# A fused attention and expert layer on one core: transposed projections, 512-column fp32 score matmuls and once-transposed tokens

## What is computed

```python
x = L0_attn_x                       # (8, 1024, 128)
xn = _layernorm(x, axis=-1)
x = x + _L0_attn_ref(xn, ...) + _L0_ffn_ref(xn, ...)
```

```python
q, k, v = (qkv[:, :, 0], qkv[:, :, 1], qkv[:, :, 2])
k = _layernorm_noaffine(k)          # over the 8 features of each head
inter = jnp.einsum('bhde,bthe->bthd', S, q_c)
scores = jnp.einsum('bthd,bshd->bhts', q_c, k_c)
scores = jnp.where(causal, scores, 0.0)
intra = jnp.einsum('bhts,bshd->bthd', scores, v_c)
S = S + jnp.einsum('bthd,bthe->bhde', v_c, k_c)
```

```python
xn = xhat[None, :, :] * ln_g[:, None, :] + ln_b[:, None, :]
h = jax.nn.relu(jnp.einsum('etd,efd->etf', xn, w1) + b1[:, None, :])
y = x[None, :, :] + jnp.einsum('etf,edf->etd', h, w2) + b2[:, None, :]
```

## Time and profile before

| | |
|---|---|
| median of 3 runs | 646.09 us (638.41 to 648.07) |
| profiled execution, its own time | 645.7 us |
| its span | 644.1 us |
| PE, PEld busy | 549.8 us (85%), 434.6 us (67%) |
| DVE, ACT, POOL busy | 396.2, 274.7, 334.3 us |
| mean granted TensorE clock | 0.919 |

### The profile page before, as it was taken

The page is one execution under the profiler, slowest core; times in us unless marked ns, Lnnn a source line. Parts: engine busy times, 40 slices in busy tenths (PEclk is TensorE's granted clock), DMA queues, the critical chain, the costliest instruction groups (busy, mean ns, idle before and its releaser), DMA issues.

```text
span 644.1 us, 18105 instructions
## 1 busy us (share of the span) xinstructions
PE 549.8 (85%) x5829; PEld 434.6 (67%) x5830; DVE 396.2 (62%) x1080; ACT 274.7 (43%) x586; POOL 334.3 (52%) x361
## 2 busy tenths in 40 slices
PE   0798588888888889889889888888979999999993
PEld 0454366666666667667767666666659899998993
DVE  5887845655556556556556456566446677777773
ACT  1688334444444443443443444444433444434341
POOL 3555135554553554544543554555105777777775
PEclk9999857997999898898897898897579999999998
DMA  9695000100100000000000000010203444444440
GB/s 231 188 292 165 0 18 19 31 26 14 31 26 13 29 29 8 29 29 8 29 29 8 29 29 8 29 31 9 52 17 51 63 59 62 56 63 60 59 58 4
DMA packets 49807, 32.08 MB, mean 50 GB/s; under 512 B 8296, under 2 KB 46440, under 8 KB 49776
## 3 DMA queue, kind: packets, MB, share of 16 engines
q0 software_dynamic: 13840, 13.93, 12.7%
q1 hardware_dynamic: 32816, 17.73, 10.5%
q10 hardware_dynamic: 3120, 0.01, 0.3%
HBM read 14.07 MB, written 18.10 MB: 50 GB/s over the span
## 4 chain that ended last, share of the span: by engine, by line
PE 76%; ACT 9%; issue 5%; DVE 3%; DMA 3%; SPq 2%; ACTq 1%; POOL 0%; POOLq 0%; DVEq 0%
PE bank L1127 13%; PE bank L1108 10%; PE bank L1246 10%; PE bank L1065 10%; PE bank L1238 5%; ACT pr L538 4%; PE bank L1096 4%; PE bank L1230 3%; PE bank L1118 3%; PE bank L1232 3%; PE bank L1231 3%; DMA resid<-in_L_attn_x_dram 3%; PE bank L1098 3%; PE bank L1141 3%; ACT q L507 2%
## 5 line engine op out<-in xcount | busy, mean ns | idle before, releaser
L343 POOL TENSOR_SCALAR_AFFINE_SELECT pr<-pr 128x512 f32<-128x512 f32 x128 | 86.4, 682 | 151.5 <-ACT pr L538 150.8
L767 DVE TENSOR_TENSOR pr<-bank,causal 128x512 f32<-128x512 f32 x128 | 87.9, 687 | 121.8 <-PE bank L1108 121.4
L410 POOL DMA_INDIRECT out_dram<-qs,idxe x72 | 112.3, 1559 | 55.5 <-DVE qs L955 29.5
L1108 PE MATMUL bank<-qqt,kkt 32*128 32x128 f16 x1024 | 91.9, 228 | 29.9 <-ACT pr L538 28.2
L543 ACT ACTIVATE y<-bank 128x128 f32<-128x128 f32 x64 | 17.7, 277 | 196.9 <-PE bank L1127 196.9
L1108 PEld LDWEIGHTS bank<-qqt,kkt 32*128 32x128 f16 x1024 | 52.4, 97 | 67.9 <-issue 28.8
L538 ACT ACTIVATE pr<-bank 128x512 f32<-128x512 f32 x128 | 77.5, 606 | 22.3 <-PE bank L1108 22.1
L1127 PE MATMUL bank<-pr,vz 128*32 128x128 f32 x2048 | 79.9, 304 | 0.4 <-POOL pr L343 0.4
L354 POOL DMA_INDIRECT slots_d<-xq,idxq x64 | 64.7, 1010 | 22.5 <-POOL idxq L349 13.0
L1246 PE MATMUL bank<-w2t,pr 128*128 x576 | 76.0, 275 | 0.0
L1065 PE MATMUL bank<-wqkv,xt 128*128 128x128 f32 x384 | 67.1, 329 | 9.8 <-ACT xt L501 9.8
(11 more groups left out here) (170 smaller groups left out, 942.1 us busy)
## 6 DMA issues: line engine op xcount, KB each, us to landing
slots_d<-zrow POOLq DMA_DIRECT2D x8, 594.0 KB, 6.4
xs<-slots_d SPq DMA_DIRECT2D x72, 66.0 KB
resid<-in_L_attn_x_dram SPq DMA_DIRECT2D x8, 512.0 KB, 6.5
out_dram<-res SPq DMA_DIRECT2D x16, 256.0 KB
state<-in_L_ffn_w_dram SPq DMA_DIRECT2D x8, 256.0 KB
res<-in_L_ffn_w_dram SPq DMA_DIRECT2D x8, 256.0 KB
out_dram<-qs,idxe POOLq DMA_INDIRECT x72
slots_d<-xq,idxq POOLq DMA_INDIRECT x64, 2.3
```

The costliest lines, as they stand in the source:

```text
L343: pool.affine_select(out=pr_v[:, i % 2, g, :, :], in_=pr_v[:, i % 2, g, :, :], compare_op=ALU.is_ge, fill=0.0, base=0, pattern=[[0, J], [1 ...
L410: pool.indirect_dma_start(out_rows, bass.IndirectOffsetOnAxis(ap=idxe[:, a:a + 1].bitcast(U32), axis=0), ye[:, a, :], None, bounds_check=N ...
L767: nc.vector.tensor_tensor(pr_v[:, a, g, :, :], SC[1][:, :].rearrange("p (j t) -> p j t", j=J), bcast(causal[:, :], 1, J), ALU.mult)\
L1108: last = mm(SC[g % 2][:, j * P:(j + 1) * P], kkt[32 * g:32 * (g + 1), i % 2, j, :], qqt[32 * g:32 * (g + 1), i % 2, j, :], start=True, sto ...
```

## The change

The kernel is written anew with the same three stages. `order` rows below are instructions of one engine in program order, as built.

Preparation. The normalised tokens go straight to `rows` (ACT 6 of the 8 tiles of a chunk, DVE 2), and every tile is transposed once into `xT`, which stays on the chip for the affinities and all projections. The expert weights leave this stage. All loads of x are issued at once, and the zeros for the slots are written behind them.

```diff
-                nc.scalar.activation(rows[:, bass.ds(c * B, B), 0:D], lnx[:, a, :, :], ACT.Copy)\
...
-            def prep(e):
-                act.wait_ge(s("w1t_ps"), e + 1)
-                nc.scalar.activation(w1tr, banks[2][:, :], ACT.Copy)
-                nc.scalar.activation(lbb, ones[:, :], ACT.Copy, scale=lb_t[:, bass.ds(e, 1)]).then_inc(s("w1tr_ready"), 1)
-                nc.scalar.activation(w1t[:, e, :], banks[2][:, :], ACT.Copy, scale=g_t[:, bass.ds(e, 1)])\
-                    .then_inc(s("w1t_ready"), 1)
...
+            def ln_norm(c):
+                act.wait_ge(s("nmr_ready"), c + 1)
+                for b in range(BY_ACT):
+                    t = c * B + b
+                    last = nc.scalar.activation(rows[:, t, 0:D], resid[:, t, :], ACT.Identity, bias=nmr[:, t:t + 1],
+                                                scale=rstd[:, t:t + 1])
```

```diff
-                nc.scalar.activation(qqt[:, a, :, :], qb16, ACT.Copy).then_inc(s("qq_sb"), 1)
-                nc.scalar.activation(pr[:, a, g, :], SC[0][:, :], ACT.Copy).then_inc(s("sc_even"), 1)
...
-            def q_low(n, par):
-                dve.wait_ge(s("q_hi"), n + 1)
-                nc.vector.tensor_tensor(qs[:, par, :, 2, :], q32[:, :].rearrange("p (h d) -> p h d", d=DK),
-                                        qs[:, par, :, 0, :], ALU.subtract).then_inc(s("q_lo"), 1)
-                dve.wait_ge(s("q_lo"), n + 1)
-                nc.vector.tensor_copy(qs[:, par, :, 1::2, :], qs[:, par, :, 0::2, :]).then_inc(s("q_parts"), 1)
-                nc.vector.tensor_copy(kkt[:, a, :, :], kb16).then_inc(s("kk_sb"), 1)
...
+            def q_expand(n, j):
+                if j == 0:
+                    act.wait_ge(s("q_ps"), n + 1)
+                    reach(act, s("sc_ps"), 4 * (n - 1))
+                nc.scalar.activation(qx[:, n % 2, :, j, :], FA[:, :].rearrange("p (i t) -> p i t", t=P), ACT.Copy,
+                                     scale=jmask[:, j:j + 1])
...
+            def score_copy(m, g):
+                if g == 0:
+                    act.wait_ge(s("sc_ps"), m + 1)
+                    reach(act, s("av_ps"), m - 1)
+                nc.scalar.activation(pr[:, m % 2, g, :], SC[g][:, :], ACT.Copy).then_inc(s("se_sb"), 1)
+                nc.scalar.activation(wts[:, WE * e:WE * e + F], FB[:, :], ACT.Copy, scale=gT[:, e:e + 1])\
...
+            def v_scale(n):
+                dve.wait_ge(s("v_ps"), n + 1)
+                dve.wait_ge(s("krs_ready"), n + 1)
+                reach(dve, s("av_ps"), 4 * (n - 1))
+                reach(dve, s("ds_ps"), n - 1)
+                nc.vector.tensor_tensor(vz_heads(n % 2, 0, HALF),
+                                        FA[:, :].rearrange("p (q j d) -> p q j d", j=J, d=DK),
+                                        bcast(krs[:, :].rearrange("p (q j) -> p q j", j=J), 3, DK),
+                                        ALU.mult).then_inc(s("v_sb"), 1)
...
+            def w2_copy(e):
+                dve.wait_ge(s("w2_ps"), e + 1)
+                nc.vector.tensor_copy(wts[:, WE * e + F:WE * (e + 1)], FA[:, :]).then_inc(s("w2_sb"), 1)
+            def b1_fold(e):
+                dve.wait_ge(s("w1_ps"), e + 1)
+                link(nc.vector.tensor_tensor(w1raw[:, e % 2, :, :], w1raw[:, e % 2, :, :], bcast(lbb[:, e, :], 1, FC),
+                                             ALU.mult))
+                link(nc.vector.tensor_reduce(out=cnt[:, 0, 0:FC], in_=w1raw[:, e % 2, :, :], axis=AX, op=ALU.add))
+                nc.vector.tensor_tensor(b1T[:, e * FC:(e + 1) * FC], smallT[:, e * FC:(e + 1) * FC], cnt[:, 0, 0:FC],
+                                        ALU.add).then_inc(s("b1_fold"), 1)
```

```diff
-                    last = mm(bank[:, i * P:(i + 1) * P], xt[:, i, :], wqkv[:, col:col + D], start=True, stop=True)
-                    qv = qs[:, par, h0:h0 + G, :, :].rearrange("p g r d -> p (g r d)")
-                    nc.tensor.transpose(qb16[:, j, :], qv, identh[:, :])
-                    kv = ks[:, par, h0:h0 + G, :, :].rearrange("p g r d -> p (g r d)")
-                    last = nc.tensor.transpose(kb16[:, j, :], kv, identh[:, :])
...
-                reach(pe, s("pr_odd" if g % 2 else "sc_even"), 2 * m + g // 2)
-                for j in range(J):
-                    last = mm(SC[g % 2][:, j * P:(j + 1) * P], kkt[32 * g:32 * (g + 1), i % 2, j, :],
-                              qqt[32 * g:32 * (g + 1), i % 2, j, :], start=True, stop=True)
...
+            def q_project(n):
+                reach(pe, s("v_sb"), n)
+                reach(pe, s("w2_sb"), (n - 1) // 2)
+                mm(FA[:, :], wqkv[:, 0:D], xT[:, HALF * n:HALF * (n + 1), :].rearrange("p i t -> p (i t)"), start=True,
+                   stop=True).then_inc(s("q_ps"), 1)
+            def kT_project(n):
+                reach(pe, s("ds_sb"), n - 1)
+                mm(FB[:, :], wqkv[:, D:2 * D], xT[:, HALF * n:HALF * (n + 1), :].rearrange("p i t -> p (i t)"), start=True,
...
+            def k_project(n):
+                pe.wait_ge(s("kT_sb"), n + 1)
+                for i in range(HALF):
+                    last = mm(FB[:, i * D:(i + 1) * D], xT[:, HALF * n + i, :], wqkv[:, D:2 * D], start=True, stop=True)
+                last.then_inc(s("kn_ps"), 1)
...
+            def state_step(n):
+                pe.wait_ge(s("kn_sb"), n + 2)
+                reach(pe, s("w1_sb"), (n + 1) // 2)
+                for i in range(HALF):
+                    last = mm(FB[:, i * P:(i + 1) * P], kn[:, n % 2, i * D:(i + 1) * D], vz_heads(n % 2, i, 1), start=True,
+                              stop=True)
...
+                reach(pe, s("se_sb"), 2 * m)
+                reach(pe, s("so_sb"), 2 * m)
+                for g in range(G):
+                    r = slice(32 * g, 32 * (g + 1))
+                    last = mm(SC[g][:, :], kT[r, n % 2, i * P:(i + 1) * P],
+                              qx[r, n % 2, i, :, :].rearrange("p j t -> p (j t)"), start=True, stop=True)
+                last.then_inc(s("sc_ps"), 1)
...
+                for j in range(J):
+                    for g in range(G):
+                        last = mm(YB[32 * g:32 * (g + 1), 0:P], vz[:, half, i, g, j, :],
+                                  pr[:, m % 2, g, j * P:(j + 1) * P], start=(n < 2 and j == 0), stop=(j == J - 1))
+                last.then_inc(s("av_ps"), 1)
```

```diff
-                reach_alone(pool, s("idx_ready"), n + 1, s("pool_passed"))
-            def scatter_rows(i, half):
-                pool.indirect_dma_start(slots_d, bass.IndirectOffsetOnAxis(ap=idxq[:, half, i:i + 1], axis=0),
-                                        xq[:, half, i, :], None, bounds_check=NS * P - 1, oob_is_err=False)\
-                    .then_inc(s(f"scattered{half}"), 16)
...
+                pool.indirect_dma_start(slots_d, bass.IndirectOffsetOnAxis(ap=pos_i[:, t:t + 1], axis=0),
+                                        rows[:, t, :], None, bounds_check=NS * P - 1, oob_is_err=False)\
...
+            sent = 0
+            for m in range(NT):
+                n, i = m // HALF, m % HALF
+                mask_scores(m, 0)
+                if m >= 8:
+                    scatter_rows(sent)
+                    sent += 1
+                mask_scores(m, 2)
+                if 8 <= m < 16:
+                    scatter_rows(sent)
+                    sent += 1
+                if i == 1 and 1 <= n < NQ - 1:
+                    state_add(n - 1)
```

```diff
-                nc.scalar.activation(xse[:, a % 2, 0, :], banks[6 + a % 2][:, 0:P], ACT.Copy).then_inc(s("sex_sb"), 1)
-                nc.scalar.activation(ht[:, a % 2, :], banks[2 + a % 2][:, :], ACT.Relu).then_inc(s("ht_sb"), 1)
-                nc.vector.scalar_tensor_tensor(out=hb[:, a % 2, :], in0=banks[a % 2][:, :], scalar=xs[:, a, D:D + 1],
-                                               in1=b1b[:, e, :], op0=ALU.mult, op1=ALU.add).then_inc(s("hb_ready"), 1)
-                mm(h, high, w1h[:, e, :], start=True, stop=False)
-                mm(h, high, w1l[:, e, :], start=False, stop=False)
-                mm(h, low, w1h[:, e, :], start=False, stop=True).then_inc(s("h_ps"), 1)
-                    last = nc.tensor.transpose(banks[2 + a % 2][:, c * P:(c + 1) * P], hb[:, a % 2, c * P:(c + 1) * P],
...
+                act.wait_ge(s("h_ps"), k + 1)
+                reach(act, s("d_ps"), k - 1)
+                for c in range(FC):
+                    last = nc.scalar.activation(ht[:, k % 2, c * P:(c + 1) * P], SC[2 + k % 2][:, c * P:(c + 1) * P],
+                                                ACT.Relu, bias=b1T[:, bass.ds(e * FC + c, 1)])
+                nc.vector.tensor_scalar(xss[:, k % 2, :], xs[:, a, 0:D], xs[:, a, D:D + 1], None, ALU.mult)\
+                nc.vector.tensor_copy(w1s[:, k % 2, :], wts[:, bass.ds(e * WE, F)]).then_inc(s("w1s_ready"), 1)
+            def se_up(k):
+                pe.wait_ge(s("sex_sb"), k + 1)
+                pe.wait_ge(s("w1s_ready"), k + 1)
+                reach(pe, s("ht_sb"), k - 1)
+                for c in range(FC):
```

(2 more changed lines are left out.)

1194 lines of the change are left out of this document (436 added, 758 removed).

## The result

The changed kernel takes 563.19 us (median of 3, 562.39 to 563.67) against 646.09: a ratio of 0.877, 95% interval 0.864 to 0.889. Timed again beside the kernel before on another chip it took 563.77, ratio 0.876 (0.8745 to 0.8782). It is faster by 12%, on the side that was predicted, but 66 us above the predicted 497 and 15 above the end of the range.

A forecast was written before the change was run, and what follows sets the result against it. PE was taken to bound attention and experts. Attention's start at 67, attention 266, first slot 5, slots 144 and a rest of 13.6 gave a span of 496, with 1.6 around it 497 us; range 465 to 548.

The forecast's parts named there:

- The strips: Attention scores: four 32-row strips run side by side in fp32, so a tile's scores take 0.96 us.
- strips in turn: Rival, attention scores: strips cannot stream together, 2.58 us more a tile, 165 in all, total 662; chance 0.04.
- neighbours only: Rival, attention scores: only neighbouring strips overlap, five rounds for two, 83 us more, total 580; chance 0.05.
- each with 0.1 for the change of shape: Attention, TensorE: streaming plus 0.1 us per shape change gives a tile of 3.49 us, 4.33 in a quad's first.
- The bank waits: Attention: TensorE waits for shared banks, 1.25 us (w1 copy) and 0.85 (w2 copy) per quad pair, 1.05 a quad.
- I take 5% instead of 11% lost: 13 us: Attention: TensorE's clock loses 5% instead of 11%, adding 13 us and making attention 266 us.
- I take 4.0 us: Preparation: a chunk takes 4.0 us, from VectorE's 3.4 and ScalarE's 3.6 to 4; routing starts at 46.
- the copy of the affinities comes ahead (0.7): Routing: the affinity copy adds 0.7 us ahead; routing takes 21 us and attention starts at 67.
- I take 2.0: Experts: a slot takes 2.0 us, 72 slots 144; bounds 1.87 and 2.35 (slow relus, late weight copy).
- Waits take over: Rival: VectorE or ScalarE late 0.7 us each tile, or slots 2.35 and attention 0.3 more a tile: 542; chance 0.14.
- What else ... stays: Experts: the 13.6 us between first product and end that are not 72 slots of 2.13 remain unchanged.
- 671 if the clock also stays at 0.89: Total for strips in turn if the granted clock also stays at 0.89: 671 us instead of 662.

The follow-up runs named there:

- one_strip: Changed kernel with all four score products of a tile on rows 0 to 31 of the array, one strip: 821.97 us.
- two_strips: Changed kernel with a tile's four score products on two strips, two on each: 617.98 us.
- bank_first: Changed kernel with VectorE's w2 copy ahead of the two score masks and ScalarE's w1 copy one tile earlier: 557.29 us.
- bank_and_v: bank_first with VectorE also scaling v ahead of folding the bias of the expert's first layer: 546.46 us.
- half_affinities: Changed kernel with nmr_one_input's edit and affinity products in one pass instead of two, on values cut to bf16: 552.75 us.
- dummy_columns: Changed kernel with one unused fp32 TensorE product of 512 columns behind each chunk's 16 affinity products: 572.35 us.
- k_copies_late: Changed kernel with VectorE's copies of the first quad's two k products behind the first part of the routing chain: 558.58 us.
- scale_ahead: Changed kernel with VectorE scaling the tokens of slot k+3 instead of slot k+2 in step k: 525.38 us.
- all_cold: Changed kernel with scale_ahead, nmr_one_input, k_copies_late, bank_and_v and VectorE's expert-number load moved behind the token scaling, no unused products: 504.33 us.
- all_half_affinities: all_cold with the one-pass affinities of half_affinities, rounded to bf16: 497.65 us.
- warm: Changed kernel with nmr_one_input's edit and unused TensorE products ahead of the first two chunks' transposes and behind each chunk's affinities: 565.11 us.
- nmr_one_input: Changed kernel with VectorE's small two-tensor operation (-mean times 1/std) replaced by six single-column operations with per-partition operands: 562.27 us.

## Why the prediction was wrong, step by step

**The strips: right.** Scores of a tile were forecast at 0.96 and took 1.07; one_strip and two_strips show that the gain rests on them. The rivals of strips in turn and of neighbours only didn't come.

**"each with 0.1 for the change of shape": mis-sized.** By the starts, a tile's score products took 1.07 (forecast 0.96), the state product 0.42 (0.32), the products with v 1.01 (1.01), the projection 0.99 (0.88), the output 0.32 (0.32). The scores and the state product cost 0.1 more than streaming and one change of shape. The projection's 0.88 had left the change out altogether, although the 0.99 of the earlier trace rows has it in. That makes the tile 3.81 instead of 3.49, 20 us in all. What the changes cost one by one wasn't tried.

**The bank waits: right in place and nearly in size.** They list 1.07 for a forecast 1.25, and 0.67 for 0.85, and taking them away brought 15.5 us where the sum had 16.8 (16 quads of 1.05). What the text missed is that one of them covered a third, the scaling of v (bank_first).

**"I take 5% instead of 11% lost: 13 us": too much.** The granted clock was 0.99 in attention, so that some 3 us were lost. So 10 of the 13 us did not come, nor 1 of the bank waits; with the 20 of the tiles attention came out 10 above. The 10 are thus a difference of errors that partly cancel. Another 2.8 us of waits that the text had at nothing lie in the last tiles, where no projection covers them (on the y copy, on a select, on the last additions); bank_and_v has them too.

**"I take 4.0 us" a chunk: failed, the largest step after the slots.** The sum had VectorE and ScalarE only. TensorE's 8 transposes and 16 affinity passes weren't put beside them. At 0.21 us a pass they are 5.0 us, with nothing left between them. Nor was POOL's addition, which holds VectorE's small operation, so that the other engines needed 4.91 and not 4.0. The affinities ended 58.9 - 46 = 13 us late: 7 by the pace of seven chunks, 4.5 behind the last transposes (50.36 to 58.9, for a forecast 4), which is TensorE's half clock alone, and 1 by a later first chunk (15.33 for 14.2). half_affinities shows it: with the passes halved and the hold gone the pace is 4.2 and the last affinity pass lies 11.7 us earlier. At full clock the same passes need 2.6 us (dummy_columns, 34.75 to 37.33) and would have been hidden behind the other engines: the step failed by leaving out the passes, their clock and the hold.

**"the copy of the affinities comes ahead (0.7)": a queue not read.** The routing's start was put where the affinities end. VectorE had two k copies ahead of them, 7 us; k_copies_late gives 5 of these back (4.6 by the time, 5.6 by the start of attention). The routing itself took 17.7 us where 21 was forecast.

**"I take 2.0" a slot: failed.** The three engines were costed, 1.87, 1.5 to 1.9 and 1.86, and they do keep 1.90 (scale_ahead). The text called it "a chain over two slots (scores copied, relu, second product)", and this was the wrong chain. The one that decided runs over VectorE's result of the slot two before and the scaling queued behind it. 72 slots of 0.38 are 27 us. The bound of 2.35, which the rival "Waits take over" has as well, is near the 2.38 that came, but by luck: it was priced from slow relus and a late weight copy, and ScalarE, the copy and POOL keep pace at 1.90. Of the signs named for this stage none came: 2.38 for 2.0, PE busy 87% for above 90%, the scatters 2.34 apart for 1.9.

**"What else ... stays": wrong by the loads.** A round costs two long slots, 1.1 and 0.6 above the others, 8 times: 13 us. The kernel before has the same loads, and there a round made one slot 0.28 longer (2.41 us, 562.86 to 565.27, for 2.13), so that the 13.6 held only 2 of these 13. The sum of the two steps, 27 and 11 us, is the stage's excess of 39.

**Where the sum ends.** With five edits, four of them to the order of a queue, all_cold takes 504 us, and all_half_affinities, which also rounds the affinities, 498, against the forecast 497. That this meets the forecast is partly luck: attention is 4 us below it, the start of attention 4 above, and the slots' 1.90 for 2.0 pays for the loads. The forecast was that of a kernel whose engines don't wait for each other's queues; the range of 465 to 548 gave 51 us for such waits, in one rival, where 66 came. One sum among the rivals doesn't come out: "671 if the clock also stays at 0.89" is about what 253 and 165 us give with 5% lost; with 11% it is some 695, by the same terms.

## What to carry to other kernels

Where three engines have nearly the same work per step, write down for each engine the order of its queue over two steps and follow one result around it; a sum of busy times gives the floor, not the time, and one operation moved by a slot was worth 38 us here. In a stage where TensorE has many small passes count them at half clock as well, whatever the stage's other engines do, and look for a second bound close behind the first. A wait that is taken away is worth only what the next late thing leaves of it: half, in the case of the two bank copies.

## What was not expected of the hardware

- TensorE's clock fell under load. With all scores on one strip PE was busy 379 of 386 us, and its granted clock was 0.81, and 0.63 in 35 us in which PE never idled; with two or four strips it was 0.99. In the preparation it fell in the middle of a run of fp32 passes of 8 columns (warm, 34 to 36 us), with idle stretches of 0.85 us only.
- A pass of 8 columns took as long as one of 128. Sixteen fp32 passes of 8 columns take 3.42 us at half clock and 1.85 at full, 0.21 and 0.11 each. Their sixteen weight loads take 3.54 and 1.87, which points at the weights; no run separates the two. Eight bf16 passes of 8 columns took 0.40 from first start to last end between transposes at half clock.
- A VectorE operation with two tensors in SBUF waits for POOL's addition: 2.04 us for 128x8 elements, and six operations with one tensor each 0.82 in the same place. The Trainium skill, page "GPSIMD Engine Reference", section "1. Specifications", has it that GpSimd's SBUF interfaces are shared with VectorE, with contention for VectorE instructions in a 2-port perf mode or with two SBUF inputs; the trace agrees on the second. Operations with one tensor were held as well: the two normalisations above, 1.62 us for 0.59, and beside POOL's memset of 3.51 us one that converts 128x128 elements to bf16, which took 3.44 (nmr_one_input, 4.05 us). Whether these ran in such a mode no run here shows.

- The load of a round's expert numbers takes 1.2 to 1.3 us on each engine, and TensorE waits about a microsecond there (0.94 and 0.99 of "issue").
